# Second and third attention of a fused transformer kernel: two units of heads at a time, six probability buffers

## The reference

```
def _attn(x, qkv_w, qkv_b, num_heads):           # second: 12 heads of 16
    q, k, v = (qkv[:, :, 0], qkv[:, :, 1], qkv[:, :, 2])
    scores = jnp.einsum('bqhd,bkhd->bhqk', q, k) * scale
    attn = jax.nn.softmax(scores, axis=-1)
    out = jnp.einsum('bhqk,bkhd->bqhd', attn, v)
    ...
def _L2_attn_ref(x, w_q, w_k, w_v, w_o, b_o):    # third: 12 heads of 64
    scores = jnp.einsum('bhnd,bhmd->bhnm', q, k) / SCALE
    attn = jax.nn.softmax(scores, axis=-1)
    h = jnp.einsum('bhnm,bhmd->bhnd', attn, v)
    ...
```

## Time and profile before

| | us |
|---|---|
| median of 3 runs | 1671.95 (1662.51 to 1679.76) |
| the profiled execution | 1669.09 |
| its span, first to last instruction | 1667.1 |
| second attention, pitch of a group | 41.0, four groups |
| third attention, pitch of a group | 64.1, four groups |
| TensorE busy over the span | 1404.5 |

### The profile page before, as it was taken

How to read it: one execution, slowest core, us unless ns; L and a number is a source line. 1 busy time by engine, 2 the same in 40 slices (tenths; PEclk the granted TensorE clock), 3 DMA queues, 4 the chain that set the end, 5 groups by cost and what they waited for, 6 DMA issues and landing times.

```text
span 1667.1 us, 31759 instructions
## 1 busy us (share of the span) xinstructions
PE 1404.5 (84%) x10300; PEld 984.7 (59%) x10300; DVE 683.6 (41%) x2124; ACT 673.0 (40%) x2261; POOL 385.9 (23%) x467
## 2 busy tenths in 40 slices
PE   6799997798566877888899899688988999889994
PEld 4566665633122434555578799454654666679993
DVE  5557756611101277444433622333542423551113
ACT  1667664410000143888842022153654643213331
POOL 5213222200000132232200266220220200124441
PEclk8999996577778778999998899799999999989997
DMA  8434331759999400000004366200000020136653
GB/s 221 138 85 125 91 97 48 232 180 365 301 311 307 140 24 1 1 0 0 0 0 128 105 200 194 75 1 1 0 0 0 16 117 0 31 107 189 187 169 105
DMA packets 96071, 178.84 MB, mean 107 GB/s; under 512 B 36570, under 2 KB 56312, under 8 KB 94336
## 3 DMA queue, kind: packets, MB, share of 16 engines
q1 hardware_dynamic: 81776, 130.75, 27.0%
q10 hardware_dynamic: 7056, 30.67, 5.6%
q0 software_dynamic: 7136, 16.10, 3.1%
HBM read 150.50 MB, written 26.99 MB: 106 GB/s over the span
## 4 chain that ended last, share of the span: by engine, by line
PE 55%; DVE 13%; issue 12%; DMA 9%; ACT 7%; SPq 2%; POOL 1%; DVEq 0%; ACTq 0%; POOLq 0%
DMA WM<-in_fc 8%; PE bank L2444 6%; PE bank L1941 6%; PE bank L2430 4%; PE bank L2014 4%; PE bank L2026 4%; PE bank L2043 3%; PE bank L1945 3%; PE bank L2434 3%; PE bank L2053 3%; PE bank L2104 2%; PE bank L1989 2%; PE bank L2096 2%; ACT ON L1674 2%; ACT KZ L1815 2%
## 5 line engine op out<-in xcount | busy, mean ns | idle before, releaser
L1941 PE MATMUL bank<-XT,AREA 128*128 128x408 f32 (+1 forms) x320 | 138.3, 557 | 23.0 <-ACT XT L1618 10.1
L2014 PE MATMUL bank<-KZ,QT 128*102 128x102 f32 x1152 | 140.2, 261 | 12.2 <-ACT PB L1674 7.4
L700 POOL TENSOR_TENSOR PB<-PB,RCU 102x306 f32<-102x306 f32 x96 | 69.3, 722 | 310.1 <-DVE RCU L964 310.0
L2014 PEld LDWEIGHTS bank<-KZ,QT 128*102 128x102 f32 x1152 | 121.0, 173 | 31.5 <-issue 15.5
L684 POOL TENSOR_TENSOR RS<-VE,expo 102x4 f32<-102x4 f32 (+1 forms) x53 | 53.1, 1002 | 361.7 <-DVE VE L904 303.6
L2444 PE MATMUL bank<-WM,KZ 128*128 x660 | 118.2, 327 | 0.0
L1941 PEld LDWEIGHTS bank<-XT,AREA 128*128 128x128 f32 (+1 forms) x320 | 56.2, 196 | 89.6 <-issue 69.4
L2444 PEld LDWEIGHTS bank<-WM,KZ 128*128 128x128 f32 x660 | 105.7, 190 | 0.4
L1655 ACT ACTIVATE KZ<-bank,AREA 128x128 f32<-128x128 f32 x198 | 54.8, 375 | 121.4 <-PE bank L2434 121.4
L2043 PE MATMUL bank<-PT,V 102*32 102x102 f32 (+1 forms) x1152 | 85.9, 270 | 15.2 <-DVE OT L974 12.3
L2026 PE MATMUL bank<-AREA,OT 128*102 128x192 f32 x384 | 88.9, 345 | 11.3 <-DVE SLOTS L1329 5.3
(11 more groups left out here) (347 smaller groups left out, 2807.3 us busy)
## 6 DMA issues: line engine op xcount, KB each, us to landing
AREA<-in_fc SPq DMA_DIRECT2D x10, 1536.0 KB, 20.3
SLOTS<-in_m3w SPq DMA_DIRECT2D x33, 384.0 KB
WM<-in_fc ACTq DMA_DIRECT2D x5, 2304.0 KB, 18.9
WM<-in_fc SPq DMA_DIRECT2D x6, 1536.0 KB, 24.1
AREA<-in_fc ACTq DMA_DIRECT2D x4, 2304.0 KB, 20.5
...
```

The source lines that it names most:

```text
L700: pool.tensor_tensor(p, p, scale, ALU.mult).then_inc(sem["probs_ready"], 1)
L1941: last = pe.matmul(dst, *whole(n), start=n < 2, stop=False)
L2014: last = pe.matmul(psum[k][0:T, cols(j)], QT[:, tile, cols(bb)], KALL[:, unit % per_tile * (HEADS // per_tile) + tile, cols(bb)], start=Tr ...
```

## The change

It touches the second and third attention only. The first keeps its code.

- **Scores.** `paired_attention` replaces `attention` on TensorE for both stages. In each even step it issues the scores of units s and s+1 in turns, head by head. The operands are only the rows of the head, 32 in the second attention and 64 in the third, and the two units lie in different rows and write to different banks. `KZ` is no longer padded: ScalarE makes one copy per bank of keys, and GpSimd's two settings of zeros and their waits go.
- **Order on TensorE.** Even step s: scores of s and s+1; values of s-6 and s-5; transposes of s-4 and s-3; then projections as before.
- **Copies of the transposes.** ScalarE copies those of even units, in front of the exponentials of unit s as before. VectorE copies those of odd units (`odd_turns`), in its odd steps, behind the inverse of unit s-1.
- **Buffers.** Six probability buffers and four transposed ones, four banks for scores, one for outputs, one bank of transposes for each of the two copying engines.
- **Values of the third attention.** They go over four banks (`VBANKS`), the two of before and the first two of the scores.

```diff
 SBANKS, TBANKS, OBANKS, XBANKS, FBANKS = (0, 1), (2, 3), (4, 5), (6, 7), (2, 3, 6, 7)
+VBANKS = OBANKS + SBANKS
...
-        SCORES, VALUES = (SBANKS + XBANKS[:1], SBANKS), (OBANKS[:1] + XBANKS[1:], OBANKS[:1])
+        SCORES, VALUES = (SBANKS + XBANKS, SBANKS), (OBANKS[:1], OBANKS[:1])
+        PTS = PT + [flat_ht[0:T, 4 * T * j:4 * T * (j + 1)].rearrange("p (h t) -> p h t", h=4) for j in range(2)]
+        PBS = PB + [flat_ht[0:T, 4 * T * j:4 * T * (j + 1)].rearrange("p (h t) -> p h t", h=4) for j in (2, 3)]
...
@@ -784,17 +787,14 @@
                     gate(place)
             gate((NG - 1) % 2)
             powers(1)
-            pool.wait_ge(sem["gated"], at.now("gated") + CT3)
-            pool.wait_ge(sem["power_out"], at.now("power_out"))
-            pool.memset(KZ[:], 0.0).then_inc(sem["halves_cleared"], at.one("halves_cleared"))
-            pool.wait_ge(sem["halves_cleared"], at.now("halves_cleared"))
...
-                    probabilities()
+                    probabilities(ring=6)
                 powers(1)
-                probabilities()
+                probabilities(ring=6)
...
-            for r in range(YRING):
-                pool.wait_ge(sem[f"scattered{r}"], 16 * len(range(r, TILES, YRING)))
-            for half in range(2):
-                pool.memset(KZ[64 - 64 * half:128 - 64 * half, half, :, :], 0.0
-                            ).then_inc(sem["halves_cleared"], at.one("halves_cleared"))
-            pool.wait_ge(sem["halves_cleared"], at.now("halves_cleared"))
...
+            def odd_turns(n):
+
+                dve.wait_ge(sem["turn_ready"], at.take("turn_ready"))
+                src = psum[TBANKS[1]][0:T, 0:TU].rearrange("p (h t) -> p h t", h=HPU)
+                give(dve.tensor_copy(PTS[n % 4][:, 0:HPU, :], src), "turn_taken")
+                dve.wait_ge(sem["turn_taken"], at.now("turn_taken"))
...
                     if 0 <= s - 1 < UNITS:
-                        inverse_sums(s - 1)
+                        inverse_sums(s - 1, 4 if pos else 6)
+                    if not pos and 0 <= s - 4 < UNITS and s % 2:
+                        odd_turns(s - 4)
...
-                    k = at.bank(OBANKS)
+                    k = at.bank(OBANKS if dv == 16 else VBANKS)
...
-                    if 0 <= s - 4 < UNITS:
-                        k = at.bank(TBANKS)
+                    if 0 <= s - 4 < UNITS and (pos or s % 2 == 0):
+                        k = at.bank(TBANKS if pos else TBANKS[:1])
                         src = full(k)[0:T, 0:TU].rearrange("p (h t) -> p h t", h=HPU)
-                        free(activation(PT[s % 2][:, 0:HPU, :], src, ACT.Copy), k)
+                        free(activation((PT[s % 2] if pos else PTS[s % 4])[:, 0:HPU, :], src, ACT.Copy), k)
                     if s < UNITS:
                         k = SCORES[bool(pos)][s % len(SCORES[bool(pos)])]
                         act.wait_ge(sem["probs_in"], at.take("probs_in"))
+                        n = s % (4 if pos else 6)
                         for j in range(HPU):
-                            p = PB[s % 4][:, j, :]
+                            p = PBS[n][:, j, :]
                             last = activation(p, p if pos else psum[k][0:T, cols(j)], ACT.Exp, scale=-1.0,
-                                              bias=MXU[:, s % 4, j:j + 1], accum_out=SMU[:, s % 4, j:j + 1])
+                                              bias=MXU[:, n, j:j + 1], accum_out=SMU[:, n, j:j + 1])
...
-                    src = full(k)[:, 0:TG]
-                    for u in range(UPB):
-                        rows = slice(32 * u, 32 * u + 32)
-                        last = activation(KALL[rows, 3 * u + j, :], src[rows], ACT.Identity,
-                                          bias=bqk1[rows, 3 + j:4 + j])
-                    free(last, k)
+                    free(activation(KT[:, j, :], full(k)[:, 0:TG], ACT.Identity, bias=bqk1[:, 3 + j:4 + j]), k)
...
-                    src = full(k)[:, 0:TG]
-                    activation(KZ[0:64, 0, p, :], src[0:64], ACT.Copy)
-                    free(activation(KZ[64:128, 1, p, :], src[64:128], ACT.Copy), k)
+                    free(activation(KT[:, p, :], full(k)[:, 0:TG], ACT.Copy), k)
...
+            def paired_attention(per_tile, dv, wo, v_moved):
...
+                def turn(n):
+
+                    pe.wait_ge(sem["probs_ready"], at.take("probs_ready"))
+                    if n % 2:
+                        k = TBANKS[1]
+                        if n == 1:
+                            pe.wait_ge(sem[f"bank_free{k}"], at.now(f"bank_full{k}") + 1)
+                        else:
+                            turned(n - 2)
+                    else:
+                        k, p = claim(TBANKS[:1])
+                    for j in range(HPU):
+                        last = pe.transpose(psum[k][0:T, cols(j)], PBS[n % 6][:, j, :], ident[0:T, 0:T])
+                    if n % 2:
+                        last.then_inc(sem["turn_ready"], at.one("turn_ready"))
+                    else:
+                        even_moved[n] = filled(last, k)
+
+                def scores(s):
+
+                    for k in (banks[s % 4], banks[s % 4 + 1]):
+                        if s < 4:
+                            pe.wait_ge(sem[f"bank_free{k}"], at.now(f"bank_full{k}") + 1)
+                        else:
+                            at.one("exp_ready")
+                    if s >= 4:
+                        pe.wait_ge(sem["exp_ready"], at.now("exp_ready"))
+                    bb = s // UPB
+                    for j in range(HPU):
+                        for unit in (s % UPB, s % UPB + 1):
+                            tile, row = unit // per_tile * HPU + j, unit % per_tile * rows_of
+                            rows = slice(row, row + rows_of)
+                            last = pe.matmul(psum[banks[bb * UPB % 4 + unit]][0:T, cols(j)], QT[rows, tile, cols(bb)],
+                                             KT[rows, tile, cols(bb)], start=True, stop=True)
+                            if j == HPU - 1:
+                                last.then_inc(sem["scores_ready"], at.one("scores_ready"))
+
+                def values(n):
+
+                    f = fill_of(dv, n)
+                    if n == 0:
+                        moved(*v_moved)
+                    turned(n)
+                    turned(n + 1)
+                    if f >= 1 and n % (UPB // fills(dv)) == 0:
+                        values_taken(f - 1)
+                    for unit in (n, n + 1):
+                        for j in range(HPU):
+                            row, rows, tile, _ = av_place(dv, HPU * (unit % UPB) + j)
+                            last = pe.matmul(psum[values_bank][row:row + rows, cols(tile)],
+                                             by_head(dv)[:, unit // UPB * HEADS + HPU * (unit % UPB) + j, :],
+                                             PTS[unit % 4][:, j, :], start=True, stop=True)
+                    if av_filled(dv, (n + 1) % UPB):
+                        last.then_inc(sem["values_ready"], 1)
+
+                for s in range(STEPS):
+                    if s < UNITS and s % 2 == 0:
+                        scores(s)
+                    if 0 <= s - 6 < UNITS and s % 2 == 0:
+                        values(s - 6)
+                    if 0 <= s - 4 < UNITS and s % 2 == 0:
+                        turn(s - 4)
+                        turn(s - 3)
...
                 xt_wide()
                 qk = []
@@ -2350,7 +2441,7 @@
-                attention(4, 16, wp1, v_moved)
+                paired_attention(4, 16, wp1, v_moved)
...
-            pe.wait_ge(sem["halves_cleared"], at.take("halves_cleared", 2))
...
-                    two_banks = [claim(OBANKS) for _ in range(2)]
+                    two_banks = [claim(VBANKS) for _ in range(2)]
...
-                attention(2, 64, wo2, v_moved[-2:])
+                paired_attention(2, 64, wo2, v_moved[-4:])
```

45 lines of the change are left out of this document (34 added, 11 removed).

## The result

| | us |
|---|---|
| median before, 20 runs | 1673.65 (1662.51 to 1686.29) |
| median after, 20 runs | 1685.39 (1676.48 to 1698.34) |
| ratio after to before | 1.0073, 95% interval 1.0048 to 1.0097 |
| the profiled execution after, its span | 1681.37, 1679.5 |

The change made the kernel about .7% slower: less than 1%, but clear of zero. The prediction was 1684. Ratios in this document are taken from fast runs alone, without those over 1.5% above the fastest of their kernel, while medians are over all runs.

A forecast was written before the change was run, and what follows sets the result against it. A closed loop of copies, exponentials, inverse, values and transposes was to set the pace. From 1669.1: second attention +7.7, third -13.6, zeros -4.0, clock +22 gave 1681.2; raised by 2.9, 1684. Range 1645 to 1702, the forecast's own 1675 to 1697.

The forecast's parts named there:

- The new cycle: Both attentions: copies, exponentials, inverse, values and transposes close a loop, 3.44 us per pair in the second, 3.63 in the third.
- Scores of .77: TensorE's scores of a pair of units, side by side in different rows, take .77 us; upper bound 1.38.
- values .47: TensorE's values of two units take .47 us in the second attention, a link of the loop.
- Third attention at full clock: Ramp and cycles cost +.9 us a group, four value banks save 4.3: net -3.4 a group, -13.6.
- Zeros: Ahead of the second attention: dropping GpSimd's first setting of KZ saves 4.0 us; the second setting saves nothing.
- The clock: TensorE's idle times in loop and ramp lower its clock: +4.5 us a group in the second attention, +1 in the third.
- signs named beforehand: Among them: PEclk under .7 in the second attention, over .9 in the third; pitches 47.4 and 61.6 us.
- By stages: Forecast changes of second attention, third attention and zeros, with the clock's share: +25.7, -9.6 and -4.0 us.
- The clock never falls: Rival: TensorE keeps full clock in both attentions despite the idle times; 1662 us, chance .20.
- The loop does not close: Rival: VectorE's copy starts early, ScalarE or TensorE with projections sets the pace; -29 us more, 1633, chance .14.
- Low throughout: Rival: the low clock holds through both attentions, dense matmuls at 1.2 GHz too; 1715 us, chance .11.
- pairs not side by side: Rival: a pair's scores take 1.38 us, still in the slack, .6 in each ramp; +5 us, no chance of its own.

The follow-up runs named there:

- the run at .96: Changed kernel, loop closed, with scores taken over all 128 rows in the same order, so only the time is read: 1664.8 us, ratio .995 to the kernel before.

## Why the prediction was right, point by point

- **The new cycle** was right in its order and its sum. 3.44 us a pair was 3.33 to 3.40 at 2.4 GHz, 4.06 was 3.94 at 1.2 GHz; exchanging two statements opened it. Scores of .77 took .72 up to the next row (1183.96 to 1184.68), values .47 stood .47 apart from the transposes behind them (700.62 to 701.09), and projections went into the slack. Predicted +1.9 us a group of the second attention at full clock, 7.7 in all; the run that all but holds it shows 43.0 against 41.0 and 7.6 in all (172.9 against 165.3), with longer scores in its ramps, so the agreement is good within a us a group and no better.
- **Third attention at full clock**: predicted -3.4 a group, thus 60.8; measured 61.2 with 128-row scores and 61.6 with doubled ones, each with a ramp that is longer by about half a us. The banks gave 3.4 as a separate part, where the prediction had 4.3 less the wait of 1.4.
- **Zeros**: -4.0 predicted, 22.7 to 18.7 measured, and back with the zeros.
- **The clock** had the right sizes on the wrong ground. Second attention: 4.5 a group predicted; measured 1.5 to 6.8 beyond the pitches of the run at .96, on average 3.8 (188.3 - 172.9, over four). Third: 1 a group predicted, from one cycle of five at the low clock; the profiled execution has just that, one cycle of 4.35 us and the others 3.52, +.8. In other executions it was more (64.4 at .87), so this size holds for the profiled one. The step that failed, though not the number, is "The new loop leaves TensorE idle for about 1.5 of every 3.44 us ... So idle times of this size do cost the clock here": with the gaps gone the second attention stayed at .73, and with the gaps left but 128-row scores it was .96 to 1.00. That the sum came out all the same is in part luck: the size was taken from the right level of the clock, 1.2 GHz in the heads and 2.4 in the dense matmuls, but the reason given would have had the clock come back once the loop was open. I had read the fall at 121.6 us in the first attention as the work of its 1.43 us gap, and didn't weigh that its records have 64 rows too. In the third attention, with 64 rows, the step holds: the ramp's gap matters once the loop is open (.86 against 1.00), and the loop's gaps once the ramp is filled (.89 against 1.00). Of the signs named beforehand, PEclk under .7 came in two groups of four (.66 to .81), and the pitches of 47.4 and 61.6 were 47.1 on average and 61.5.
- **By stages**: +25.7, -9.6 and -4.0 us predicted with the clock's share; +23.0, -10.6 and -4.0 measured, 8.4 together where 12.1 was forecast. The median moved by 11.7; the other stretches of the profiled executions differ by +4.1 together, within what they differ by there from one execution to another.
- **Rivals.** "The clock never falls", 1662: the run with 128-row scores and the loop closed gave 1664.8. "The loop does not close", 1633: it did close; opened, it gave 1664.9 with the low clock and 1639.6 with the high one, so that rival's price was right only with a condition that it didn't name. Low throughout, and pairs not side by side, didn't occur; made by hand the latter went with 16 us and not 5, nearly all of it a clock that stayed low for longer. (The price of "low throughout" adds up to 1712, 1684 and four times 7, and not to 1715.)
- **The Trainium skill**, TensorEngine Tiling (Array Packing), "PSUM Bottleneck", warned that with smaller tiles the emptying of PSUM may become what bounds. Here the changed kernel ran at 3.33 us a pair and more, and with the loop open TensorE set the pace at 1.2 GHz. Only with the loop open and 128-row scores did ScalarE come near its 2.23 us: two copies of even units stand 2.28 us apart (719.25 and 721.53), and over 715 to 733 us it was busy 16.3 of 18 us, as TensorE was. Of "Mode switching requires drain" (Key Properties of the same page of the Trainium skill) these rows show no separate price; the scores came out at .72 where the estimate was .77.
